# A graph and mixture-of-experts layer: the last six experts in a loop on TensorE, the last matrix in five column blocks

## What is computed

```python
def moe_forward(x, gate_w, expert_bias, w_up, w_down, shared_w_up, shared_w_down):
    ...
    h = _masked_grouped_mm(routed_in.astype(jnp.bfloat16), w_up.astype(jnp.bfloat16), onehot)
    h = jnp.square(jax.nn.relu(h.astype(jnp.bfloat16)))
    routed_out = _masked_grouped_mm(h.astype(jnp.bfloat16), w_down.astype(jnp.bfloat16), onehot)
    ...
    hs = jnp.square(jax.nn.relu(xf @ shared_w_up.T))
    shared_out = hs @ shared_w_down.T
    out = combined.reshape(-1, TOP_K, dim).sum(axis=1) + shared_out
```

## Time and profile before

| | us |
|---|---|
| median of 3 runs | 359.8 (359.49 to 360.01) |
| the profiled execution, its own time | 359.56 |
| its span, first to last instruction | 358.2 |
| PE busy | 310.8 (87% of the span) |
| PE's load of weights busy | 148.2 |
| VectorE, ScalarE, POOL busy | 110.7, 58.2, 45.6 |
| mean granted clock of TensorE | 0.952 of full |
| moved by DMA | 104.92 MB |

### The profile page before, as it was taken

One profiled execution on the slowest core, in us unless ns is written; L12 is line 12 of the kernel. 1 busy time (PEld: TensorE's weight loads), 2 busy tenths in 40 slices (PEclk: granted clock), 3 DMA queues, 4 the chain that ended last, 5 costly groups with the idle time before them and its releaser, 6 DMA issues.

```text
span 358.2 us, 2956 instructions
## 1 busy us (share of the span) xinstructions
PE 310.8 (87%) x1192; PEld 148.2 (41%) x1192; DVE 110.7 (31%) x242; ACT 58.2 (16%) x109; POOL 45.6 (13%) x84
## 2 busy tenths in 40 slices
PE   4999998999999999999879998899898864384667
PEld 4334334334343343533234565533454532142334
DVE  7608504501143439400822313200322330111111
ACT  1401000001003010300020033300323330120131
POOL 0611111111212111222300000000001030000000
PEclk9999999999999999999989999999999995866888
DMA  7999999999999999999999999999999999999996
GB/s 291 365 299 295 425 276 422 269 425 327 388 330 346 378 318 429 266 422 317 293 358 270 292 419 339 224 209 219 216 216 224 206 228 211 209 229 204 215 211 136
DMA packets 12425, 104.92 MB, mean 293 GB/s; under 512 B 1504, under 2 KB 1976, under 8 KB 3068
## 3 DMA queue, kind: packets, MB, share of 16 engines
q0 software_dynamic: 10944, 98.57, 95.5%
q1 hardware_dynamic: 1168, 6.01, 4.3%
q10 hardware_dynamic: 300, 0.16, 0.2%
HBM read 150.48 MB, written 0.39 MB: 421 GB/s over the span
## 4 chain that ended last, share of the span: by engine, by line
PE 64%; DMA 24%; DVE 4%; issue 4%; another core or an unknown queue 2%; ACT 2%; DVEq 0%
PE bank L832 30%; DMA stage<-in_expert_down 10%; PE bank L1010 10%; PE bank L990 8%; PE bank L968 6%; PE bank L1046 5%; DMA ring<-in_mat_wik 5%; DMA ring<-in_mat_wk 4%; DMA ring<-in_mat_mv 4%; PE bank L956 1%; PE bank L801 1%; ACT hbuf L440 1%; PE bank L816 1%; ACT xn L434 1%
## 5 line engine op out<-in xcount | busy, mean ns | idle before, releaser
L832 PE MATMUL bank<-ring,xnt 128*96 128x512 f32 x224 | 100.4, 606 | 1.1 <-ACT xnt L370 0.6
L832 PEld LDWEIGHTS bank<-ring,xnt 128*96 128x96 f32 x224 | 36.6, 166 | 59.7 <-issue 56.9
L1010 PE MATMUL bank<-stage,hbuf 128*96 128x512 bf16 (+3 forms) x198 | 46.2, 394 | 17.2 <-DMA stage<-in_expert_down 14.3
L990 PE MATMUL bank<-stage,late 128*96 128x512 bf16 (+1 forms) x192 | 44.7, 387 | 10.8 <-issue 10.3
L832 PE MATMUL bank<-ring,stage 128*96 128x512 f32 x96 | 42.1, 593 | 0.1
L1010 PEld LDWEIGHTS bank<-stage,hbuf 128*96 128x96 bf16 x198 | 24.4, 135 | 36.8 <-DMA stage<-in_expert_down 15.9
L990 PEld LDWEIGHTS bank<-stage,late 128*96 128x96 bf16 x192 | 24.2, 131 | 28.1 <-issue 16.4
L776 DVE TENSOR_TENSOR acc<-acc_t,acc 96x512 f32<-96x512 bf16 (+3 forms) x18 | 11.3, 628 | 58.9 <-ACT acc_t L459 58.7
L434 ACT ACTIVATE xn<-bank 96x512 bf16<-96x512 f32 (+2 forms) x26 | 14.5, 559 | 66.0 <-PE bank L990 59.8
L832 PEld LDWEIGHTS bank<-ring,stage 128*96 128x96 f32 x96 | 15.3, 163 | 23.2 <-issue 23.2
L763 DVE TENSOR_TENSOR xn<-xn 96x512 bf16<-96x512 bf16 (+1 forms) x24 | 9.6, 400 | 45.1 <-ACT xn L434 45.1
(11 more groups left out here) (161 smaller groups left out, 202.9 us busy)
## 6 DMA issues: line engine op xcount, KB each, us to landing
stage<-in_expert_up POOLq DMA_DIRECT2D x4, 2816.0 KB, 32.4
stage<-in_expert_down POOLq DMA_DIRECT2D x4, 2816.0 KB, 38.9
stage<-in_expert_down POOLq DMA_DIRECT2D x7, 1408.0 KB, 17.4
stage<-in_expert_up POOLq DMA_DIRECT2D x6, 1024.0 KB, 12.8
ring<-in_shared_down POOLq DMA_DIRECT2D x2, 2816.0 KB, 14.4
ring<-in_shared_up POOLq DMA_DIRECT2D x5, 1024.0 KB, 17.2
ring<-in_mat_wq SPq DMA_DIRECT2D x4, 1024.0 KB, 9.5
ring<-in_mat_wv POOLq DMA_DIRECT2D x4, 1024.0 KB, 11.7
```

Source lines behind the costliest of these rows:

```text
L832: ins = mm(bank[BANKS[m] + h][0:N, :], tiles(src)[:, k, :], w[:, kk, :], start=(k == 0), stop=(k == KT - 1))
L990: ins = mm(bank[4 + j][0:N, 0:c1 - c0], tiles(xe)[:, k, :], w[:, k, :], start=(k == 0), stop=(k == KT - 1))
L1010: ins = mm(bank[j][0:N, 0:c1 - c0], tiles(e_h)[:, t, :], w[:, t, :], start=(t == 0), stop=(t == TT - 1))
```

## The change

On PE experts 2 to 7 become the body of a hardware loop of two rounds (`pe.Fori(0, 2)`): experts 2, 3, 4 in the first, 5, 6, 7 in the second. All waits in the body compare with values worked out from the loop's counter. So that the two rounds have one shape, expert 4 gets the same blocks as expert 7, and the semaphores of landings are regrouped: `up_landed` and `down_landed` for each buffer, and `part_landed` for parts, of which the first loads of experts 0 and 1 use each once. PE waits for these ahead of experts 0 and 1 (five more waits). Expert 4's matrices are still loaded whole.

`FINE` becomes five blocks of 336, 288, 208, 128 and 64 columns, and expert 7's down matrix is loaded in five parts. The fifth block uses bank 0 again and waits for the copy of the first. There are still four stores; the first covers two blocks (624 columns). Expert 2's down product waits for both adds of the shared product for either bank. The last wait on `out_taken` at the end of PE's program is new.

```diff
@@ -50,15 +50,21 @@
 HALVES = [(0, 512), (512, 1024)]
-FINE = [(0, 512), (512, 832), (832, 960), (960, 1024)]
+FINE = [(0, 336), (336, 624), (624, 832), (832, 960), (960, 1024)]
 EARLY = 6
-FINE_CUTS = [0, 512 * TT, 832 * TT, 960 * TT + EARLY * 64, D * TT]
-BLOCKS = [HALVES] * (EXPERTS - 1) + [FINE]
-FIRST_LOADS = [(e, 0, t0, t1, 0) if m == 0 else (e, 1, t0, t1, 1) for e in range(3)
-               for m, t0, t1 in [(0, 0, 4), (0, 4, 8), (0, 8, 11), (1, 0, HALF * TT), (1, HALF * TT, D * TT)]]
+FINE_CUTS = [0, 336 * TT, 624 * TT, 832 * TT, 960 * TT + EARLY * 64, D * TT]
+STORES = [0, 624, 832, 960, 1024]
+BLOCKS = [FINE if e in (4, 7) else HALVES for e in range(EXPERTS)]
+DOWN_BEFORE = [0, 2, 6, 8, 10, 15, 17, 19, 24]
+OUT_BEFORE = [0, 2, 4, 6, 8, 13, 15, 17]
+ROUND = 9
+FIRST_LOADS = [(e, m, x0, x1) for e in range(3) for m, x0, x1 in
+               [(0, 0, 4), (0, 4, 8), (0, 8, 11), (1, 0, HALF * TT), (1, HALF * TT, D * TT)]]
 FIRST_AT = [0, 1, 2, 7, 11, 17, 20, 22, 27, 33, 37, 39, 40, 43, 44]
@@ -182,7 +188,14 @@
         sh_dn_landed = [sem(f"sh_dn_landed{j}") for j in range(2)]
-        stage_landed = [[sem(f"stage_landed{b}_{j}") for j in range(3 + len(FINE) if b == 1 else 2)] for b in range(3)]
+        up_landed = [sem(f"up_landed{b}") for b in range(3)]
+        down_landed = [sem(f"down_landed{b}") for b in range(3)]
+        part_landed = [sem(f"part_landed{j}") for j in range(len(FINE))]
+        FIRST_LANDED = [up_landed[0], up_landed[0], part_landed[4], part_landed[2], part_landed[3],
+                        up_landed[1], up_landed[1], part_landed[0], down_landed[1], part_landed[1],
+                        up_landed[2], up_landed[2], up_landed[2], down_landed[2], down_landed[2]]
         out_landed = sem("out_landed")
@@ -251,10 +264,6 @@
-        def down_before(e):
-            return e * len(HALVES) + (len(HALVES) if e >= 2 else 0)
@@ -288,20 +297,20 @@
-            for j, (c0, c1) in enumerate(FINE[:-1]):
-                sp.wait_ge(added, down_before(EXPERTS - 1) + j + 1)
+            for j, (c0, c1) in enumerate(zip(STORES[:-2], STORES[1:-1])):
+                sp.wait_ge(added, DOWN_BEFORE[EXPERTS - 1] + j + 2)
                 sp.dma_start(out[:, c0:c1], acc[0:N, c0:c1])\
                   .then_inc(out_landed, 16)
-            sp.wait_ge(out_landed, 16 * len(FINE))
+            sp.wait_ge(out_landed, 16 * (len(STORES) - 1))
...
         def _(pool):
-            def load(e, m, x0, x1, j):
+            def load(e, m, x0, x1, landed):
                 b = e % 3
...
                 pool.dma_start(place[:, f0:f1], (expert_up, expert_down)[m][e, :, f0:f1])\
-                    .then_inc(stage_landed[b][j], 16)
+                    .then_inc(landed, 16)
@@ -311,7 +320,7 @@
             piece_landed(pool, 1)
-            load(*FIRST_LOADS[0])
+            load(*FIRST_LOADS[0], FIRST_LANDED[0])
             pool.wait_ge(bias_v_landed, 16)
@@ -334,7 +343,7 @@
                             pool.wait_ge(mvec_t_psum, 2)
-                        load(*FIRST_LOADS[n])
+                        load(*FIRST_LOADS[n], FIRST_LANDED[n])
@@ -343,15 +352,16 @@
                 pool.wait_ge(up_done, up_before(e - 3) + PARTS)
-                load(e, 0, 0, TT, 0)
-                pool.wait_ge(down_done, down_before(e - 3) + len(HALVES))
-                load(e, 1, 0, D * TT, 1)
+                load(e, 0, 0, TT, up_landed[e % 3])
+                pool.wait_ge(down_done, DOWN_BEFORE[e - 3] + len(HALVES))
+                load(e, 1, 0, D * TT, down_landed[e % 3])
             e = EXPERTS - 1
-            pool.wait_ge(down_done, down_before(e - 3) + len(HALVES))
-            load(e, 0, 0, 8, 0)
-            load(e, 0, 8, TT, 2)
-            for j in range(len(FINE)):
-                load(e, 1, FINE_CUTS[j], FINE_CUTS[j + 1], 3 + j)
+            pool.wait_ge(down_done, DOWN_BEFORE[e - 3] + len(FINE))
+            load(e, 0, 0, 8, up_landed[1])
+            load(e, 0, 8, TT, part_landed[0])
+            load(e, 1, FINE_CUTS[0], FINE_CUTS[1], down_landed[1])
+            for j in range(1, len(FINE)):
+                load(e, 1, FINE_CUTS[j], FINE_CUTS[j + 1], part_landed[j])
@@ -448,7 +458,7 @@
-                done = down_before(e)
+                done = DOWN_BEFORE[e]
                 if e:
@@ -456,13 +466,13 @@
                     act.wait_ge(down_done, done + j + 1)
-                    nc.scalar.activation(rounded[:, c0:c1], bank[j][0:N, 0:c1 - c0],
+                    nc.scalar.activation(rounded[:, c0:c1], bank[j % 4][0:N, 0:c1 - c0],
                                          ACT.Copy).then_inc(out_taken, 1)
...
                 expert(e)
-            c0, c1 = FINE[-1]
-            act.wait_ge(added, down_before(EXPERTS - 1) + len(FINE))
+            c0, c1 = STORES[-2:]
+            act.wait_ge(added, DOWN_BEFORE[EXPERTS - 1] + len(FINE))
             act.dma_start(out[:, c0:c1], acc[0:N, c0:c1]).then_inc(out_landed, 16)
@@ -770,9 +780,9 @@
                 if e:
-                    dve.wait_ge(added, down_before(e))
+                    dve.wait_ge(added, DOWN_BEFORE[e])
                 for j, (c0, c1) in enumerate(BLOCKS[e]):
-                    dve.wait_ge(out_taken, e * len(HALVES) + j + 1)
+                    dve.wait_ge(out_taken, OUT_BEFORE[e] + j + 1)
                     tt(acc[0:N, c0:c1], rounded[:, c0:c1], acc[0:N, c0:c1], ALU.add)\
@@ -969,20 +979,17 @@
-            def expert(e, freed):
-                b, turn, blocks = e % 3, e // 3, BLOCKS[e]
+            def expert(e, b, blocks, ups, downs, parts, freed, out0):
                 up = stage[b][:, 0:TT * UNIT // 2].bitcast(BF16)
...
                 for j, (c0, c1) in enumerate(UP_COLS):
                     if j == 0:
-                        pe.wait_ge(stage_landed[b][0], turn * 16 + 48)
-                    if j == PARTS - 1 and blocks is FINE:
-                        pe.wait_ge(stage_landed[b][2], 16)
+                        pe.wait_ge(up_landed[b], ups)
+                    if j == PARTS - 1 and parts is not None:
+                        pe.wait_ge(part_landed[0], parts)
@@ -994,20 +1001,21 @@
                 for j, (c0, c1) in enumerate(blocks):
-                    if blocks is FINE and j < len(FINE) - 1:
-                        pe.wait_ge(stage_landed[b][3 + j], 16)
-                    if blocks is HALVES and j == 0:
-                        pe.wait_ge(stage_landed[b][1], turn * 16 + 32)
+                    if j == 0 and downs is not None:
+                        pe.wait_ge(down_landed[b], downs)
+                    if blocks is FINE and 0 < j < len(FINE) - 1:
+                        pe.wait_ge(part_landed[j], parts)
                     if freed is not None and j < len(HALVES):
-                        pe.wait_ge(freed, 2 * len(HALVES) + j + 1 if e == 2 else
-                                   (e - 1) * len(HALVES) + j + 1)
+                        pe.wait_ge(freed[0], freed[1 + j])
                     if j == 0:
                         pe.wait_ge(ht_ready, up0 + PARTS)
+                    if j == 4:
+                        pe.wait_ge(out_taken, out0 + 1)
                     w = down[:, c0 * TT:c1 * TT].rearrange("p (t c) -> p t c", t=TT)
...
                         if blocks is FINE and j == len(FINE) - 1 and t == EARLY:
-                            pe.wait_ge(stage_landed[b][3 + j], 16)
-                        ins = mm(bank[j][0:N, 0:c1 - c0], tiles(e_h)[:, t, :], w[:, t, :],
+                            pe.wait_ge(part_landed[j], parts)
+                        ins = mm(bank[j % 4][0:N, 0:c1 - c0], tiles(e_h)[:, t, :], w[:, t, :],
                                  start=(t == 0), stop=(t == TT - 1))
@@ -1034,8 +1042,12 @@
             pe.wait_ge(ht_ready, PARTS)
-            expert(0, None)
-            expert(1, out_taken)
+            for j in (2, 3, 4):
+                pe.wait_ge(part_landed[j], 16)
+            expert(0, 0, HALVES, 32, None, None, None, None)
+            for j in (0, 1):
+                pe.wait_ge(part_landed[j], 16)
+            expert(1, 1, HALVES, 32, 16, None, (out_taken, 1, 2), None)
@@ -1046,10 +1058,15 @@
                 ins.then_inc(down_done, 1)
-            expert(2, added)
-            for e in range(3, EXPERTS):
-                expert(e, out_taken)
+            with pe.Fori(0, 2) as i:
+                at, turn = i * ROUND, i * 16
+                expert(i * 3 + 2, 2, HALVES, turn + 48, turn + 32, None, (added, at + 6, at + 6), None)
+                expert(i * 3 + 3, 0, HALVES, turn + 48, turn + 16, None,
+                       (out_taken, at + 5, at + 6), None)
+                expert(i * 3 + 4, 1, FINE, turn + 48, turn + 32, turn + 16,
+                       (out_taken, at + 7, at + 8), at + 8)
+            pe.wait_ge(out_taken, OUT_BEFORE[EXPERTS - 1] + len(FINE))
 def kernel(**inputs):
```

## The result

The changed kernel takes 358.62 us, the median of 22 runs (358.32 to 359.73); the kernel before took 359.74 in the same sets, also 22 runs (359.45 to 360.47). The ratio is 0.9974, 95% interval 0.9968 to 0.9980: 1.12 us or 0.3% less, small but clear of no change. The prediction said 360.1, from 358.8 to 361.3, and gave "faster" a chance of 0.2.

What follows compares the result with a forecast made beforehand. The prediction took the DMA queue to bound the bf16 experts, the end being the third block's landing plus 3.3 us; 359.56 + 0.1 + 0.2 + 0.15 = 360.0, with the median 0.24 above given as 360.1, range 358.8 to 361.3.

Steps and rivals of the forecast that it cites:

- (c): PE's loop: every product issued as before, expert 4's extra 1.0 us hidden by waiting, register steps in the tail +0.15.
- rival 1: Code queue: second round runs from code already there, expert 7's late packet goes, 1.2 us saved, about 358.7; chance 0.2.
- the 0.24 of the median: Whole kernel: the profiled execution, 359.56 us, lies 0.24 under the median of 359.8, so 0.24 is added.
- the rule of the Trainium skill: Loop branch: a taken branch whose target is outside a two-page window must fetch it by DMA before going on.
- (a): Cuts of expert 7's down matrix: one more transfer costs 0 to 0.1 us, 0.1 taken; finer start gains nothing.
- (b): Clock in the tail: gaps may lower it, the last 22 products taking 1.76 us for 1.29; half of +0.47, +0.2.
- the register steps: Tail, between the third landing's wait and the fifth block's two: 0 to 0.4 us, 0.15 taken.
- The cover: Before expert 5's down product: 6.9 us of waiting, in which up to 6 us of late start vanish.
- (d): Stores at the end: still four, the first with 624 columns; no gain, up to +0.3 us, 0 taken.
- Rival 2: Code reloaded in the second round: two packets on one already late engine delay expert 7's landings 1.2 us, 361.2; chance 0.2.
- Rival 3: Slow tail: low clock and dear register steps together, 360.5, up to 361.0 with stores and median; chance 0.15.

Runs made afterwards that it cites:

- the run with eleven packets: The kernel before, all code written out, with an alignment ahead of the code of experts 5, 6 and 7: 360.06 us, ratio 1.0007.
- the products in the gaps: Changed kernel with 8, 8 and 4 unread products added after the last down product's first three blocks: 358.48 us; with last cut after 2 tiles too, 358.29 and 358.15.
- that kernel (358.27): The changed kernel with the last cut after 2 tiles of the 64-column block in place of 6: 358.27 us, ratio 0.9956.
- the upper cluster: Six of the changed kernel's 22 runs, with nothing changed between runs: 359.42 to 359.73 us.
- the lower cluster: Sixteen of the changed kernel's 22 runs, with nothing changed between runs: 358.32 to 358.80 us.

## Why the prediction was wrong

**The step that failed is (c), "what runs is no less".** It counted the instructions that PE executes, and in the sum the packets that carry them got no term. The loop makes the static code smaller, and the packet that made expert 7 late went with it: −1.0 to −1.2 us (10.86 to 9.68; 10.65 to 9.65 between two kernels that differ in the loop). The mechanism was worked out as rival 1, from the same 10.86 us and nine packets, with 358.7, which came true. That it came out to 0.1 is partly luck: it has 0.25 for the cut and the loop, which measured about 0, and leaves out the 0.24 of the median. What was wrong there was the chance. It was held down to 0.2 on two grounds. One was that PE would have to keep the whole body; the rule of the Trainium skill says it doesn't, and the runs say it does, up to some seven blocks. The other was that nothing in the rows shows a branch. The lateness itself was in rows, and a rule that no row could support should not have outweighed it. The range left out the time of its own rival 1. A slip besides: 359.56 + 0.45 + 0.24 is 360.25, not 360.1.

(a) *The cut*: +0.1 taken; the blocks alone moved the 128-column block by 0.04 us (354.94 for 354.90). That "the finer start gains nothing in this run" held. It might have a use where the clock is low: with the old blocks PE then worked through from 348.56 to 356.60 in 44 products (the run with eleven packets). No run shows such a gain, and with the loop the old blocks were as fast (358.53).

(b) *The clock*: right in kind for a quarter of the executions, and the size off. I had +0.47 for 22 products and half of it in the forecast. When the clock is low it is low for the 208-column block too, which then ends after the 128 columns have landed: 33 products in 4.17 us, done at 355.98. With the products in the gaps and the clock at 1.00 the 22 started at 353.63 and ended at 354.92; the loss is 1.06, and 359.31 is 1.04 above the median of that kernel (358.27). In the median execution it is 0, and in a quarter some 1.05.

(c) *The rest of the loop*: the register steps cost nothing in the tail (22 products in 1.29, before and after; 0.15 taken). Expert 4's down product in five blocks took 5.16 us for 4.92, +0.24 and not +1.0: the prediction added up times of blocks that stood alone, and back to back they took less. The cover held: expert 5's up product started at 288.40, 0.83 later than before, and its down product still waited.

(d) *Stores*: nothing seen, as taken.

Rival 2 (more packets, 361.2) didn't come up. The price that it put on two packets wasn't tested: in the run with eleven they held up three different engines. Rival 3 exists in part as the upper cluster, some 1.05 above the lower.

The sum with the measured terms: 359.56 − 1.0 to −1.2 + 0.04 + 0 + 0 is 358.4 to 358.6; the lower cluster is 358.3 to 358.8.

## What to carry to other kernels

Where a transfer queue is the bound to the end, code is traffic too: count the packets in the instruction queue, and look for a landing later than the bytes before it explain. A packet costs something only if it makes its engine the last of the 16: here the one at 332 cost 1.2 us, the one at 292 nothing. So a fetch block less in the static code of the busiest engine can be worth a packet's time, and a move of code alone can lose or win as much. A hardware loop saves blocks if its body stays within what the engine keeps (some seven blocks for PE here); beyond that it was far worse than writing out the code (384.13 us). When a stall that is worth the whole change is in the rows and only a remembered rule speaks against its going, give that case the larger chance. Look at the spread of the runs as well: a low clock in the last 5 us cost 1 us in the one such execution profiled, and with a few products in the gaps none of 16 runs was so long.

## What the hardware did that I had not expected

- PE ran a loop over two or three blocks of code twice without a packet in the second round, and one over about seven too; with nine or ten it had eleven packets from 302 us on and took 384.13 us.
- One packet of 16 KB among 2 MB of data, 0.6% of the share of 16 engines in its window, made one engine of 16 the last and moved all later landings by 1.0 to 1.2 us; two further ones made two other engines as late, and from expert 7 on moved none.
- The same kernel with the last cut earlier has executions 1.05 us apart; in the long one every transfer was on time, and the clock was 0.50 in the last 5 us.
